# Routing in four groups with fixed regions of rows per expert, and a first attention that begins with one sequence's loads

## The reference

```
x = x + attention0(layernorm(x))   # 16 heads of 16, rope, causal softmax
x = x + moe0(layernorm(x))         # 8 experts, best 2, gelu, 1024 hidden
x = x + attention1(layernorm(x))   # cosine attention and an MLP
x = x + moe1(layernorm(x))         # 64 experts, best 8, and 2 shared

# moe0
logits = xf @ gate_w                       # 4096 x 8
top_w, top_idx = top_k(logits, 2);  top_w = softmax(top_w)
out = sum over the 2 experts of  top_w * (gelu(xf @ w1 + b1) @ w2 + b2)
```

## Time and profile before

| what | us |
|---|---|
| median of 3 runs | 3064.24 (3055.07 to 3066.49) |
| the profiled execution, its own time | 3059.81 |
| its span in the trace | 3058.1 |
| TensorE busy in the span | 2517.8 |
| first attention, from its loads to its end | 0 to 709.3 |
| routing up to the first scatter | 709.3 to 797.3 |
| scatters, up to the expert phase | 797.3 to 884.5 |

### The profile page before, as it was taken

One profiled execution on the slowest core, in us unless ns is written; L12 is line 12 of the kernel. 1 busy time (PEld: TensorE's weight loads), 2 busy tenths in 40 slices (PEclk: granted clock), 3 DMA queues, 4 the chain that ended last, 5 costly groups with the idle time before them and its releaser, 6 DMA issues. The chain is left out here.

```text
span 3058.1 us, 50413 instructions
## 1 busy us (share of the span) xinstructions
PE 2517.8 (82%) x18511; PEld 2196.2 (72%) x18511; DVE 1787.3 (58%) x3152; ACT 1330.8 (44%) x2053; POOL 810.6 (27%) x1143
## 2 busy tenths in 40 slices
PE   1988888885229999973677778877999999999999
PEld 1777676774229999972466566666888888988988
DVE  5555555544228888866877777726744544444444
ACT  0444444542017776753333334333444444444444
POOL 3444444401430000014566564541000000000000
PEclk9799999987559999995789899998999999999999
DMA  2000000004137676755555454404422222222222
GB/s 83 1 2 2 2 1 2 2 1 140 58 134 242 228 242 226 239 177 149 140 126 133 130 135 120 133 28 142 131 93 83 87 83 87 83 83 82 92 75 87
DMA packets 191373, 312.26 MB, mean 102 GB/s; under 512 B 28308, under 2 KB 100184, under 8 KB 191192
## 3 DMA queue, kind: packets, MB, share of 16 engines
q1 hardware_dynamic: 179112, 272.01, 29.2%
q0 software_dynamic: 12080, 37.76, 3.7%
HBM read 269.84 MB, written 39.85 MB: 101 GB/s over the span
## 5 line engine op out<-in xcount | busy, mean ns | idle before, releaser
L2143 DVE TENSOR_TENSOR e_h_lo<-e_h,e_h_hi 128x512 fp32r<-128x512 f32 x320 | 221.5, 692 | 476.0 <-ACT e_h_hi L2219 475.9
L2205 ACT ACTIVATE e_h<-e_h_ps,e_b 128x512 f32<-128x512 f32 x320 | 219.9, 688 | 494.8 <-PE e_h_ps L2284 476.7
L2300 PE MATMUL e_y_ps<-e_w_hi,e_h_hi 128*128 128x256 f32 x1280 | 363.7, 284 | 15.2 <-DVE e_h_lo L2143 15.1
L2300 PE MATMUL e_y_ps<-e_w_hi,e_h_lo 128*128 128x256 f32 x1280 | 358.6, 280 | 0.0
L2300 PE MATMUL e_y_ps<-e_w_lo,e_h_hi 128*128 128x256 f32 x1280 | 357.8, 280 | 0.0
L2300 PEld LDWEIGHTS e_y_ps<-e_w_hi,e_h_hi 128*128 128x128 f32 x1280 | 240.2, 188 | 40.0 <-DVE e_h_lo L2143 24.9
L2284 PE MATMUL e_h_ps<-e_yT_hi,e_w_hi 128*128 128x512 f32 x640 | 257.3, 402 | 1.5 <-ACT e_h L2205 0.6
L402 DVE TENSOR_REDUCE a_top<-a_ring 128x2 f32<-128x1024 f32 (+3 forms) x256 | 202.8, 819 | 89.6 <-PE a_ring L603 88.7
L2284 PE MATMUL e_h_ps<-e_yT_hi,e_w_lo 128*128 128x512 f32 x640 | 253.7, 396 | 0.0
L2284 PE MATMUL e_h_ps<-e_yT_lo,e_w_hi 128*128 128x512 f32 x640 | 253.3, 396 | 0.0
L2300 PEld LDWEIGHTS e_y_ps<-e_w_lo,e_h_hi 128*128 128x128 f32 x1280 | 240.5, 188 | 13.2
(11 more groups left out here) (360 smaller groups left out, 6914.3 us busy)
## 6 DMA issues: line engine op xcount, KB each, us to landing
e_w<-in_w SPq DMA_DIRECT2D x78, 1024.0 KB, 5.4
e_spread<-share_store SPq DMA_DIRECT2D x512, 128.0 KB, 2.8
a_keys<-rows_store SPq DMA_DIRECT2D x128, 256.0 KB, 5.1
a_queries<-rows_store SPq DMA_DIRECT2D x86, 256.0 KB, 4.5
a_running_hidden<-rows_store SPq DMA_DIRECT2D x42, 256.0 KB, 4.4
sorted_x<-zeros POOLq DMA_DIRECT2D x10, 1024.0 KB, 16.9
e_xs<-sorted_x SPq DMA_DIRECT2D x39, 256.0 KB, 5.0
sorted_y<-e_ys POOLq DMA_DIRECT2D x39, 256.0 KB, 5.7
```

The lines of the kernel that those rows point to most:

```text
L2143: dve.tensor_tensor(h_parts[q % 2][1][:, :], h[:, q % 2, :], h_parts[q % 2][0][:, :], ALU.subtract).then_inc(h_lo.sem, h_lo.tick())
L2205: act.activation(h[:, q % 2, :], h_ps[q % 2][:, :], ACT.Silu, bias=b1[:, c:c + 1]).then_inc(h_ready.sem, h_ready.tick())
L2300: last = pe.matmul(y_ps[n][:, 0:D], h_parts[q % 2][a][:, n * P:(n + 1) * P], w2[b][:, c, :], start=(q == 0 and m == 0), stop=(q == CH - 1 ...
```

## The change

**Start.** x is loaded in three batches, `BATCHES`: sequence 0, sequence 1, sequences 2 to 7, each with its own semaphore. The first is ahead of all, wqkv, the identity and wproj next (`loaded`, 3 loads), then bias and rope loads (`rest_loaded`), batch 1, the constants (`const_loaded`), batch 2. Statistics, seed and refinement are done by batch: batch 0 ahead of `norm(0)`; batch 1 on DVE between `low_parts(0)` and `biased`, on POOL behind `add_bias(0)`; batch 2 in the body of sequence 0, four tiles ahead of each `a2` for r = 0 to 5, the seed ahead of that for r = 6, and on POOL behind sequence 1's stack tiles. `constants()` is moved behind `biased` on DVE. TensorE transposes once the 3 loads are there.

**Regions.** Expert e's rows start at e * 4096, so a row number is known as soon as the tokens up to it are counted. `sorted_x` and `sorted_y` grow from 40 to 136 blocks of 256 rows. Zeros are written in the first attention: 16 DMAs of SP from `heads_T` (cleared by DVE) to the first 4096 rows of `sorted_x`, then 17 DMAs which copy these over the rest of `sorted_x` and over `sorted_y`. SP waits for them at its end; ScalarE waits for the 16 ahead of its first write to `heads_T`.

**Routing by group.** Four groups of 8 tiles. `g.y` is written by DVE directly. `find_ranks` sums the counts of earlier tiles by matmuls (16 per group), `head` carries the counts from group to group. POOL scatters a group as its rows are there. `slot_block` gives each slot's block, with some steps more on DVE at the end, and is read by SP and POOL in a register for each slot.

```diff
         @block.sync
...
+            load_x(0)
             for dst, src in (
-                (g.x[:, :, :], t["x"].rearrange("b (n p) d -> p (b n) d", p=P)),
+                (w_raw, t["wqkv"].rearrange("(c p) n -> p c n", p=P)),
                 (g.ident[:, :], t["ident"][:, :]),
-                (w_raw, t["wqkv"].rearrange("(c p) n -> p c n", p=P)),
                 (wp_raw, t["wproj"].rearrange("(c p) n -> p c n", p=P)),
+            ):
+                sp.dma_start(dst, src).then_inc(loaded.sem, loaded.tick(16))
...
+            load_x(1)
...
+            load_x(2)
+
+            sp.wait_ge(zeros_ready.sem, zeros_ready.at(1))
+            zeros = heads_T[:, :].rearrange("p (n d) -> p n d", d=D)
+            step = zeros.shape[1] * P
+            for at in range(0, TOKENS, step):
+                sp.dma_start(t["sorted_x"][at:at + step, :].rearrange("(n p) d -> p n d", p=P), zeros).then_inc(zeroed.sem,
+                        zeroed.tick(16))
+            sp.wait_ge(zeroed.sem, zeroed.at(zeroed.n))
+            for rows, start in (("sorted_x", TOKENS), ("sorted_y", 0)):
+                for at in range(start, BLOCKS * SLOT_TOKENS, TOKENS):
+                    size = min(TOKENS, BLOCKS * SLOT_TOKENS - at)
+                    dst, src = (t[name][a:a + size, :].rearrange("(p r) d -> p (r d)", p=P)
+                                for name, a in ((rows, at), ("sorted_x", 0)))
+                    sp.dma_start(dst, src).then_inc(spread_zeros.sem, spread_zeros.tick(16))
+            sp.wait_ge(spread_zeros.sem, spread_zeros.at(spread_zeros.n))
...
             def prepare():
+                dve.wait_ge(refined.sem, refined.at(12))
                 norm(0)
                 low_parts(0, 0)
+                dve.wait_ge(x_loaded[1].sem, x_loaded[1].at(16))
+                statistics(range(*BATCHES[1]))
+                seed(1)
+                dve.wait_ge(rest_loaded.sem, rest_loaded.at(4 * 16))
                 for n in range(TB):
                     biased(0, 0, n, (1 + n) % 3)
+                constants()
...
+                    if not before and what == "a2":
+
+                        if r == 0:
+                            dve.wait_ge(x_loaded[2].sem, x_loaded[2].at(16))
+                        if r < B - 2:
+                            statistics(range((r + 2) * TB, (r + 3) * TB))
+                        elif r == B - 2:
+                            seed(2)
...
+REGION = TOKENS // SLOT_TOKENS
+BLOCKS = E0 * REGION + SLOTS + 1 - 2 * REGION
...
+            refine(0)
+            refine(1)
+            scatter(0)
+            refine(2)
+            scatter(1)
+            refine(3)
+            scatter(2)
+            scatter(3)
             pool.wait_ge(written.sem, written.at(written.n))
...
+            normalise(0)
+            for q in range(GROUPS):
+                if q + 1 < GROUPS:
+                    statistics(q + 1)
+                low_parts(q)
+                choose(q)
+                if q + 1 < GROUPS:
+                    normalise(q + 1)
+                place(q)
...
+            def find_ranks(q):
+                pe.wait_ge(picked.sem, picked.at(q + 1))
+                if q:
+                    pe.wait_ge(rank_taken.sem, rank_taken.at(q))
+                pe.matmul(rank_ps[:, 0:GT * E0], tri[:, :], both[:, :, :].rearrange("p n e -> p (n e)"), start=True, stop=False)
+                for n in range(GT - 1):
+                    pe.matmul(rank_ps[:, (n + 1) * E0:GT * E0].rearrange("p (n e) -> p n e", e=E0), ones[:, :],
+                              both[:, n:n + 1, :].broadcast_to([P, GT - 1 - n, E0]), start=False, stop=(n == GT - 2))
+                for n in range(GT):
+                    last = pe.matmul(count_ps[:, 0:E0], ones[:, :], both[:, n, :], start=(n == 0), stop=(n == GT - 1))
+                last.then_inc(ranked.sem, ranked.tick())
...
+            pe.wait_ge(split.sem, split.at(7))
+            turn(0)
+            for q in range(GROUPS):
+                find_logits(q)
+                if q + 1 < GROUPS:
+                    turn(q + 1)
+                find_ranks(q)
...
             e = sp.value_load(g.slot_expert[0:1, bass.ds(slot, 1)], min_val=0, max_val=E0 - 1)
+            at = sp.value_load(g.slot_block[0:1, bass.ds(slot, 1)], min_val=0, max_val=BLOCKS - 1)
             free("x")
```

More of the change, by code:

```diff
@@ L294, in body @@
                     turn_step.close()
+                if not before:
+                    refine(2)
             turns(pool, prepare, body, lambda: None)
@@ new lines, in _, with statistics, seed @@
+            dve.memset(heads_T[:, :], 0.0).then_inc(zeros_ready.sem, zeros_ready.tick())
+            def statistics(tiles):
+                for n in tiles:
+                    dve.bn_stats(stats[:, n, :], g.x[:, n, :]).then_inc(stat_step.sem, stat_step.tick())
+            def seed(batch):
+                a, b = BATCHES[batch]
+                dve.wait_ge(stat_step.sem, stat_step.at(stat_step.n))
+                dve.tensor_copy(half[:, a:a + 1], stats[:, a, 0:1]).then_inc(stat_step.sem, stat_step.tick())
+                for n in range(a, b):
+                    dve.bn_aggr(mv[:, n, :], stats[:, n, :]).then_inc(stat_step.sem, stat_step.tick())
+                dve.wait_ge(stat_step.sem, stat_step.at(stat_step.n))
+                dve.tensor_scalar(var[:, a:b], mv[:, a:b, 1], EPS, None, ALU.add).then_inc(stat_step.sem, stat_step.tick())
+                dve.wait_ge(stat_step.sem, stat_step.at(stat_step.n))
+                dve.tensor_scalar(half[:, a:b], var[:, a:b], 0.5, None, ALU.mult).then_inc(stat_step.sem, stat_step.tick())
+                rsqrt_seed(dve, stat_step, None, rstd[:, a:b], var[:, a:b])
+                assert stat_step.n == SEEDED[batch]
@@ L385, in body @@
             def body(s, m, before, more):
+                if not before:
+                    dve.wait_ge(refined.sem, refined.at(2 * 12))
                 if more:
@@ L423, in body @@
                                                   DH0]), ALU.mult).then_inc(heads_taken.sem, heads_taken.tick())
+                if not before:
+                    dve.wait_ge(refined.sem, refined.at(3 * 12))
                 dve.wait_ge(max_turned.sem, max_turned.at(PAIRS, s))
@@ L468, in body @@
                         act.wait_ge(heads_done.sem, heads_done.at(group + 1, s))
+                        if not before and not group:
+                            act.wait_ge(zeroed.sem, zeroed.at(zeroed.n))
                         if group:
@@ L896, in _, with turn @@
             act.wait_ge(exp_step.sem, exp_step.at(1))
[L897 removed]
+            act.activation(g.share[1][:, :], apart[:, :], ACT.Exp).then_inc(exp_step.sem, exp_step.tick())
         @block.tensor
         def _(pe):
[L901 to L904 removed]
+            def turn(q):
+                for j in range(2):
+                    pe.wait_ge(y_ready.sem, y_ready.at(q * GT + (j + 1) * TB))
+                    if q:
+                        pe.wait_ge(lo_ready.sem, lo_ready.at((2 * (q - 1) + j + 1) * KC))
@@ L912, in _, with find_logits @@
+                        last.then_inc(turned.sem, turned.tick())
+            def find_logits(q):
+                for j in range(2):
+                    pe.wait_ge(lo_ready.sem, lo_ready.at((2 * q + j + 1) * KC))
+                    if q:
+                        pe.wait_ge(logits_taken.sem, logits_taken.at(2 * (q - 1) + j + 1))
                     for n in range(TB):
```

441 lines of the change are left out of this document (214 added, 227 removed).

## The result

Four runs of the changed kernel had a median of 3016.1 us (3010.7 to 3016.6), beside 3061.8 us before: a ratio of 0.9857, 95% interval 0.9828 to 0.9887. It is 45.7 us faster; 51.9 were forecast, 3012 us in a range of 2996 to 3034. The span of the profiled execution fell from 3058.1 to 3014.7 us, by 43.4.

A forecast was written before the change was run, and what follows sets the result against it. TensorE, busy 82% of the span, leaves time only where it stands still. Start and attention 27.3 plus routing 26.4, less 1.5 and 0.3, gives 51.9 us off 3059.8, 3012 on the median's scale; range 2996 to 3034.

The forecast's parts named there:

- The start: Ahead of the first attention: first xn at 14.2 us, 31.2 earlier; TensorE's loop at 49.9, 29.3 earlier.
- Statistics in the first sequence: First attention body: 24 more statistics and a seed on DVE, 10.7 us, mostly covered by idle time; 2 taken.
- Zeroing: SP's copies during attention: 67.1 MB in some 203 us counted once, 407 counted twice, ending at 250 to 450, hidden.
- The chain of scatters: Routing: POOL's 64 scatters in lots of 16, two idle stretches of 8.2 us behind refinements; expert phase 26.4 us earlier.
- my signs of being wrong: Scatters over 1.1 us, TensorE waits over 5 for nothing, copies past 600, or normalise(2) held by logits, not its refinement.
- From the last scatter to the expert phase: End of routing: 4.3 us, as before, putting the expert phase 148.8 us behind the routing's start, where it was 175.2.
- Scatter slowdown: Routing: 1.5 us added for all scatters that run beside a busy DVE, 1.08 us each instead of 0.96.
- rival A: Routing: DVE holds POOL's scatters up, by its copies, casts and scalar steps; 3018 to 3026 us, chance 0.15.
- Rivals B: First sequence pays up to 10.7 us for statistics, or loads land later at the start; 3020 to 3035, chance 0.12.
- C: Zeroing copies not done when attention ends, SP's last wait keeps the stage open; 3214 us at 80 GB/s, chance 0.04.
- E: Routing steps shorter than counted, or POOL's two idle stretches of 8.2 us don't arise; down to 2996, chance 0.06.
- D: TensorE's code loads at loop jumps wait behind the zeroing copies; 3025 to 3037 us, chance 0.10.

The follow-up runs named there:

- changed_again: The changed kernel, unaltered, profiled once more on another chip: 3003.8 us, beside 3057.5 for the kernel before.
- all_ahead: Changed kernel with routing statistics and refinement of groups 0 to 2 in the last attention body, group 3's behind group 0's low parts, normalisation before choosing: 2971.2 us.
- copies_late: Changed kernel with SP's 17 zeroing copies held back until the fourth sequence's projection is added, some 280 us later: 3011.5 us.

## Why the prediction was right, point by point

- **The start** (31.2 us to the first xn, 29.3 to the loop): 30.9 and 28.9. POOL's refinement took 5.7 us where 3.4 was taken, DVE's seed was ready at 8.7 instead of 9.0. The sequence-1 statistics lay in DVE's wait, as said.
- **Statistics in the first sequence** ("I take 2", bounds 0 and 10.7): 2.9 us of TensorE's idle time. The attention ended 33.7 us earlier instead of 27.3 in the first profile and 31.1 in changed_again; equal attention work differs by 7.5 to 10 us between traces, by the clock, so that the 6.4 us are within luck.
- **Zeroing** ("counted once, 203 us"): 67.1 MB from 38 to near 240 us at some 332 GB/s. Written 100.66 MB against 39.85, hidden.
- **First scatter at 37.1**: 37.7, 37.6 and 37.6.
- **The chain of scatters** (lots at 69.3, 101.5 and 121.7, end 141.9, with a gap 144.5): changed_again has 68.1, 98.6, 118.9 and 139.1, the last two lots back to back, each idle stretch of 7.0 and 7.2 us behind a refinement and DVE waiting for that refinement 3.3 us. The first profile has 71.4, 105.3, 129.2 and 149.2: there one of my signs of being wrong came true: normalise(2) was held by the logits and not by its refinement, by 3.0 us.
- **From the last scatter to the expert phase, 4.3**: 7.65 in every kernel with the changed routing. The gap of 2.6 us that I carried over from before didn't come back.
- **Experts' first register load, 0.3**: e_w's load was issued 2.1 us into the phase instead of 0.95, 1.15 us.
- **Scatter slowdown, 1.5, and rival A**: 64 scatters took 0.967 us in the mean while DVE worked 41 us beside them, 0.96 without. Rival A is out. The Trainium skill (SBUF — State Buffer, Who interferes with whom) would have those of DVE's copies and scalar steps that use both ports block them; no row here shows it beyond the 1.01 us of a lot's first scatter, all_ahead least, where 33 us of DVE's work fell into 80.9 us of scatters at their full pace. Which of the steps used both ports no row tells, so the rule is not tested by this.
- **Rivals B, C, E** didn't come: the copies were done some 435 us ahead of the attention's end, and both idle stretches arose. **D** didn't come, but its mechanism is there (8.4 and 9.3 us beside copies, 3.1 to 4.6 in the other traces' jumps). The Trainium skill (Runtime: NRT & Kernel Launch, Instruction fetch mechanics) states that a taken branch out of the loaded pages waits for a transfer of code; the packets in the waits of copies_late and of after agree.

The sum against its own time: 33.7 for the start and attention (27.3), 18.4 to the expert phase (26.4 less 1.5), less 8.7 behind it (0.3): 43.4 where 51.9 stood. In changed_again it is 31.1 + 28.5 - 3.6 = 56.0. The step that failed in the first profile is the routing's 26.4: late signals, 10 us, which no row of before could show, as TensorE had nothing to do there beside scatters; without them it is 28.5. That the total came within 4 us of 3012 in spite of this is luck in part: the start and attention gave 6.4 us more than their term, which hid the routing's 6.5 us less, and what is behind lost 8.4 more than its 0.3, of which 1.15 is the register load and the rest at least in part the clock.

## What to carry to other kernels

When work is spread over a slow chain of one engine, look at what else stands in that engine's queue: here moving two refinements of 3.3 us by eight scatters ended the scatters 13.5 us earlier (about half of it by signals that were no longer late), and taking them and DVE's statistics out of the routing, with the next group normalised before choosing, raised the gain from 46 us, or 54 in the one run without late signals, to 86. A first item that comes 50 us sooner is worth only as much as the chain behind it is kept fed. Idle time of an engine covers added work only until its waits reach TensorE's; here 8 us more of it then cost 14.5, most of them at a lower clock. And before a gain of 10 us is put down to a change, profile the same kernel twice, on more than one chip.

## What the runs showed of the hardware

- TensorE's signal to DVE came up to 6.7 us after its last recorded matmul in three of five jobs, only beside scatters. With more matmuls behind it, it stayed the same in groups 1 and 2. There it came 2.5 to 2.7 us behind the end of the lot's last scatter; whether the scatters' end released it was not tried. Whether TensorE finished late or its signal travelled late, and what on the chip makes it so, is open; the Trainium skill (Perfetto Trace Analysis, Tensor Engine Instruction) says that the ends of TensorE's instructions are modelled in such a trace. The same five traces also lack records of semaphore updates: of the 292 updates that the routing's instructions on TensorE and DVE make, 25 have no record in after, 20 to 48 in the other four; of the seven traces without late signals six lack none and all_ahead one. So the two go together, and what lies behind both is open.
- POOL's drain at the end of the routing took 5.28 us in all twelve traces with the changed routing and 1.94 in the two with the old one, whatever the order of the scatters. Its cause was not tried.
- Stalls of up to 2.5 us on TensorE in the first body went with a granted clock of 0.74 instead of 0.86: the matmuls took 11.5 us more where the stalls themselves grew by 3.0. The clock of equal work also moved by itself: 0.83 for 0.97 over 50 us in two traces of one kernel.
- A copy within DRAM moved at 325 to 336 GB/s at full share, each byte counted once, and slowed nothing on the engines but a jump's code load.
